# Attention in a transformer layer: the ones and value matmuls of two key tiles issued together, ones first, after one wait

## What is computed

```python
def attn(x):                                  # x is layer-normed
    qkv = x @ Wqkv                            # q: 32 heads x 128, k: 128, v: 128
    scores = einsum('bqhd,bkd->bhqk', q, k) * 128 ** -0.5
    alibi = slopes[h] * (pos_k - pos_q)       # slopes fall from head 0 to head 31
    scores = where(pos_k <= pos_q, scores + alibi, -1e30)
    return einsum('bhqk,bkd->bqhd', softmax(scores), v) @ Wo
x = x + layernorm(attn(layernorm(x)))
# feed-forward: three 4096 x 4096 layers with weights +1 / -1 made of booleans
h = relu(s0 * (layernorm(x) @ pm(k0))) * 2
h = relu(s1 * (ei(h) @ pm(k1))) * 2           # ei: the last 819 features times -4
x = x + layernorm(s2 * (ei(h) @ pm(k2)))
```

## Time and profile before

| | us |
|---|---|
| median of two runs | 7135.25 |
| the two runs | 7068.7 and 7201.79 |
| the profiled execution | 7065.34 |
| its span, from the first to the last instruction on the slowest core (core 1) | 7063.8 |
| spans of the other seven cores | 7047.1 to 7061.9 |
| mean granted TensorE clock, all cores | 0.906 to 0.911 of full speed |

### The profile page before, as it was taken

How to read it: one execution, slowest core, us unless ns; L and a number is a source line. 1 busy time by engine, 2 the same in 40 slices (tenths; PEclk the granted TensorE clock), 3 DMA queues, 4 the chain that set the end, 5 groups by cost and what they waited for, 6 DMA issues and landing times. The chain is left out here.

```text
span 7063.8 us, 68459 instructions; the slowest of 8 cores (7047.1 to 7063.8 us)
## 1 busy us (share of the span) xinstructions
PE 5567.9 (79%) x26898; PEld 2564.7 (36%) x26898; DVE 1513.9 (21%) x1592; ACT 1714.4 (24%) x3454; POOL 416.0 (6%) x492
## 2 busy tenths in 40 slices
PE   1998678981799999990299868888981799999990
PEld 1444333430344444440144423444431344444440
DVE  3001671015110110004300123441015110110004
ACT  3001650005100100003300298881005100100004
POOL 0000000000011110000000000000000011110000
PEclk9999999995899999995599989999995899999995
DMA  2543003442344443324344300004542344443324
GB/s 50 77 72 54 1 1 61 77 72 70 65 78 72 75 78 72 78 66 141 61 72 76 45 1 1 1 1 60 74 75 64 70 75 72 78 75 75 76 68 143
DMA packets 491400, 445.22 MB, mean 63 GB/s; under 512 B 9683, under 2 KB 476628, under 8 KB 480852
## 3 DMA queue, kind: packets, MB, share of 16 engines
q0 software_dynamic: 478848, 373.32, 31.3%
q1 hardware_dynamic: 12244, 67.53, 2.8%
HBM read 461.78 MB, written 50.33 MB: 72 GB/s over the span
## 5 line engine op out<-in xcount | busy, mean ns | idle before, releaser
L397 PE MATMUL pb<-wst,A 128*128 128x512 bf16 (+1 forms) x12800 | 2729.3, 376 | 119.7 <-DMA wst<-wo 29.2
L397 PEld LDWEIGHTS pb<-wst,A 128*128 128x128 bf16 x12800 | 1251.8, 98 | 1596.6 <-issue 159.8
L605 ACT ACTIVATE PTs<-pb,eb_sb 128x64 bf16<-128x64 f32 (+4 forms) x2720 | 941.2, 621 | 251.2 <-PE pb L547 151.6
L807 PE MATMUL pb<-Bt,wst 128*128 128x512 bf16 x4096 | 890.1, 381 | 17.1 <-DVE wst L780 17.1
L807 PE MATMUL pb<-A,wst 128*128 128x512 bf16 x4096 | 889.7, 381 | 13.4 <-DVE wst L780 13.3
L505 PE MATMUL pb<-PTs,on 128*128 128x512 bf16 (+2 forms) x1280 | 466.0, 364 | 167.7 <-ACT PTs L605 163.3
L807 PEld LDWEIGHTS pb<-Bt,wst 128*128 128x128 bf16 x4096 | 402.0, 98 | 505.2 <-issue 25.8
L807 PEld LDWEIGHTS pb<-A,wst 128*128 128x128 bf16 x4096 | 401.7, 98 | 500.9 <-issue 21.3
L547 PE MATMUL pb<-QT,KT 128*128 128x512 bf16 (+2 forms) x1280 | 453.0, 370 | 106.8 <-DVE QT L584 72.8
L572 DVE RECIPROCAL DR<-pb 128x512 f32<-128x512 f32 x128 | 429.1, 3352 | 291.3 <-PE pb L510 291.3
L510 PE MATMUL pb<-PTs,Vb 128*128 128x512 bf16 (+2 forms) x1280 | 466.7, 365 | 0.0
(11 more groups left out here) (66 smaller groups left out, 2127.9 us busy)
## 6 DMA issues: line engine op xcount, KB each, us to landing
wst<-k POOLq DMA_DIRECT2D x256, 512.0 KB, 4.2
wst<-wqkv POOLq DMA_DIRECT2D x64, 1024.0 KB, 8.4
wst<-wo POOLq DMA_DIRECT2D x64, 1024.0 KB, 9.5
wst<-k POOLq DMA_DIRECT2D x64, 1024.0 KB, 5.8
oh<-x POOLq DMA_DIRECT2D x32, 1024.0 KB, 9.4
out<-oh SPq DMA_DIRECT2D x32, 1024.0 KB, 6.1
x1sp<-Bt SPq DMA_DIRECT2D x16, 1024.0 KB, 4.3
ln<-x1sp SPq DMA_DIRECT2D x32, 512.0 KB, 5.6
```

Of the source, the lines that this page charges most:

```text
L397: mi = t.matmul(pb[tl][:, 0:Wd], lhsT_get(i, tl), wst[:, n % 2, ii, 0:Wd], start=(i == 0), stop=(i == 31))
L605: i = s.activation(PTs[:, j % 4, off:off + w], pb[4 + j % 3][:, off:off + w], AF.Exp, bias=eb[:, col:col + 1])
L807: mi = t.matmul(pb[pbase + 2 * oc + sh][:, 0:512], wst[:, n % 2, ii, oc * 128:oc * 128 + 128], arena_chunk(src_arena, i)[:, sh * 512: sh * ...
```

## The change

`emit_dpv` is replaced by `emit_dpv_group`, which takes two trips. It waits once, for the exponentials of the later trip of the two, then issues both ones matmuls, then both value matmuls. Trips are collected in the list `pend`, and a group is issued as soon as four are pending, that is behind every second score matmul. What is left at the end of a head is issued in groups of two. The operands, banks, buffers and the number of matmuls stay what they were, and so does every other engine's program.

```diff
-            def emit_dpv(t, j):
-                ...
-                t.wait_ge(sEXP.sem, bEXP + j + 1)
-                di = t.matmul(pb[2 + n % 2][:, qs:512], on1[:, :],
-                              PTs[:, j % 4, 0:Wd], ...)
-                if j == head_last[h]:
-                    di.then_inc(sQf.sem, 1)
-                mi = t.matmul(pb[n % 2][:, qs:512], Vb[:, kt, :],
-                              PTs[:, j % 4, 0:Wd], ...)
-                mi.then_inc(sPV.sem, 1)
+            def emit_dpv_group(t, js):
+                t.wait_ge(sEXP.sem, bEXP + js[-1] + 1)
+                for j in js:
+                    ...
+                    di = t.matmul(pb[2 + n % 2][:, qs:512], on1[:, :],
+                                  PTs[:, j % 4, 0:Wd], ...)
+                    if j == head_last[h]:
+                        di.then_inc(sQf.sem, 1)
+                for j in js:
+                    ...
+                    mi = t.matmul(pb[n % 2][:, qs:512], Vb[:, kt, :],
+                                  PTs[:, j % 4, 0:Wd], ...)
+                    mi.then_inc(sPV.sem, 1)
...
-                        jh0 = j
+                        pend = []
...
                                 mi.then_inc(sST.sem, 1)
-                                if j > jh0 + 1:
-                                    emit_dpv(t, j - 2)
+                                pend.append(j)
+                                if len(pend) >= 4:
+                                    emit_dpv_group(t, [pend.pop(0),
+                                                       pend.pop(0)])
                                 j += 1
-                        if j > jh0 + 1:
-                            emit_dpv(t, j - 2)
-                        emit_dpv(t, j - 1)
+                        while pend:
+                            emit_dpv_group(t, pend[:2])
+                            pend = pend[2:]
```

More of the change, by code:

```diff
@@ L498, in trip_parts @@
                 return h, qloc, kt, qq, qs, Wd, subs, n
-            def emit_dpv(t, j):
-                h, qloc, kt, qq, qs, Wd, subs, n = trip_parts(j)
-                nkt = 4 * qq + 4
-                km = _ktmin(h, qq)
-                t.wait_ge(sEXP.sem, bEXP + j + 1)
-                di = t.matmul(pb[2 + n % 2][:, qs:512], on1[:, :],
-                              PTs[:, j % 4, 0:Wd],
-                              start=(kt == km), stop=(kt == nkt - 1))
-                if j == head_last[h]:
-                    di.then_inc(sQf.sem, 1)
-                mi = t.matmul(pb[n % 2][:, qs:512], Vb[:, kt, :],
-                              PTs[:, j % 4, 0:Wd],
-                              start=(kt == km), stop=(kt == nkt - 1))
-                mi.then_inc(sPV.sem, 1)
+            def emit_dpv_group(t, js):
+                t.wait_ge(sEXP.sem, bEXP + js[-1] + 1)
+                for j in js:
+                    h, qloc, kt, qq, qs, Wd, subs, n = trip_parts(j)
+                    nkt = 4 * qq + 4
+                    km = _ktmin(h, qq)
+                    di = t.matmul(pb[2 + n % 2][:, qs:512], on1[:, :],
+                                  PTs[:, j % 4, 0:Wd],
+                                  start=(kt == km), stop=(kt == nkt - 1))
+                    if j == head_last[h]:
+                        di.then_inc(sQf.sem, 1)
+                for j in js:
+                    h, qloc, kt, qq, qs, Wd, subs, n = trip_parts(j)
+                    nkt = 4 * qq + 4
+                    km = _ktmin(h, qq)
+                    mi = t.matmul(pb[n % 2][:, qs:512], Vb[:, kt, :],
+                                  PTs[:, j % 4, 0:Wd],
+                                  start=(kt == km), stop=(kt == nkt - 1))
+                    mi.then_inc(sPV.sem, 1)
             with nc.Block() as blk:
```

## The result

The changed kernel is slower: 1.0070 times the kernel before, 95% interval 1.0057 to 1.0084, that is 49 us (40 to 59) on the 7068.7 of the faster run before. This is well under the 2% above which the forecast would have called it slower. The forecast was 70 us, which lies above the interval. The profiled execution took 7122.06 us, 57 over that of before.

A forecast was written before the change was run, and what follows sets the result against it. The prediction took ScalarE to pace attention's first heads and TensorE the last twenty of the second half; 57 us at the same clock plus 13 for the clock gave 7135, or 7139 against the faster run, range 7110 to 7180.

The forecast's parts named there:

- The bound of each stage: Second-half attention: ScalarE paces the first heads, TensorE heads 12 to 31; first-half heads 12 to 31: VectorE's evacuations delay turns.
- Part 1, the shared stationary: Two ones matmuls of a group load the same matrix: taken as 0, bounds 0 and a gain of 64 us.
- Part 2, the second exponential: Second-half heads 12 to 31: waiting for two exponentials makes every second group 0.21 us late; 1.6 a head, 32 us.
- First half, heads 12 to 31: VectorE's evacuation wait absorbs the loss at a head's start; 0.4 us a head remains, 8 us for 20 heads.
- Heads 8 to 11: Loop of 3.09 us for four trips against 2.92; 1.85 us a head in second half, 0.5 in first, 9 us.
- Heads 0 to 7: ScalarE never runs dry in the stream; 0.6 us a head in second half, 0.4 in first, 8 us.
- Part 3, the clock: Heads 12 to 31: added idle time lowers TensorE's granted clock; 13 us taken, bounds 0 and 39 us more.
- The sum: Whole kernel: 57 us at the same clock plus 13 us for the clock, 70 us on 7065.3, giving 7135.
- Hidden: Rival: ScalarE hop 0.2 us shorter in the stream, late groups vanish, some 25 us stay: 7090; chance 0.13.
- Faster by fewer waits: Rival: each TensorE wait before ones matmuls costs a fixed price, half go, 84 us less: 6985; chance 0.04.
- Clock: Rival: added idle drops attention's clock, to 0.91 in second half, 0.76 in first; 119 us in all, 7188; chance 0.21.

The follow-up runs named there:

- e3: Changed kernel with its single wait kept, but ones and value matmuls alternating (D P D P) within the group; 7118.3 us at best, no interval.
- e1: Changed kernel with its order kept, but each ones matmul waits for its own trip's exponentials alone; 7075.1 us in one execution.
- e4: Kernel before with its order kept, but the first ones matmul of each pair waits for the later trip's exponentials; 1.0342 times the kernel before, 7300 us.
- e6: Changed kernel with groups issued at six pending trips instead of four and eight exponential buffers instead of four; 1.0060 times the kernel before.
- e8: Changed kernel with the wait for VectorE's evacuation moved to a query block's first ones matmul, as in e5; 1.0024 times the kernel before.
- e9: Changed kernel's groups in one stream across heads, evacuation wait at the first ones matmul; 0.9897 times the kernel before.
- e5: Kernel before with the wait for VectorE's evacuation moved from a query block's first score matmul to its first ones matmul; 0.9924 times the kernel before.

## Why the prediction was right, point by point

**The bound of each stage** was read rightly. The late heads of the second half carry 37 of the 64 us in the profile, the ones bound by ScalarE (heads 0 to 7 there) 5.

**Part 1, the shared stationary, 0.** Right, and e3 tests it apart from the rest: 21.41 us with D P D P, 21.42 with D D P P.

**Part 2, the second exponential.** Forecast for a second-half head of tier 512: five late groups of 0.21, two starts of 0.36, 0.2 given back, 19.77 to 21.4. Measured 21.42, with each piece at its place in the timeline: 0.36 late at the start and again at the turn, five late groups (0.22 us three times and 0.26 twice, the latter where the tiles are narrow, 1.2 in all), and the 0.22 us wait before the head's last D gone. Taking the wait back removes 1.40 of 1.65 us (e1), putting the wait alone into the old order makes a clean head 26.02 (e4), and giving the loop two more trips makes 20.20 (e6). In total 20 x 1.65 = 33 us, forecast 32.

**First half, heads 12 to 31.** Forecast 0.4 a head, measured 11.52 - 11.13 = 0.39. That VectorE's wait takes in a part of the price is shown by e8, and in the head itself: the wait at the turn, 1.51 us before, is now

```profile
863.89 0.59 PE L552 MATMUL pb<-QT,KT 128*128 128x512 bf16 x2 [1.15 <-DVE A L582]
```

It is shorter by 0.36, what the start loses.

**Heads 8 to 11.** Forecast 7.4 and 2 us, measured 6.5 and 1.0.

**Heads 0 to 7.** Forecast 8 us in all, measured 3.5 + 1.9 in the second half and 2.4 + 6.5 in the first, 14. The second half fits (5 forecast); heads 0 to 3 of the first half lost 6.5 us where 1.6 was put. On this core the time at half clock rose there from 35 to 52 us, and the forecast had looked for the clock only in heads 12 to 31. But the clock is only a part of it: on cores 2, 4 and 6 that time was 45 us before and 41 to 45 after, and the same heads lost 3.2 to 3.6 us all the same. So some 3 us are the clock and some 3 a cost that the forecast put at 1.6; what it consists of is open.

**Part 3, the clock, 13 us.** The direction was right. In heads 12 to 31 of the second half the clock now falls in 9 of 20, nearly every second head, before in 5 (6 to 9 and 1 to 5 over the cores). Two neighbouring heads after, 20 and 22 us of them:

```profile
4571.00:4591.00 20.00, 17.57 (x87) 7.73 (x88) 8.65 (x5) 16.11 (x28) 0.00 (x0) 1.00 0.00 0
4592.00:4614.00 22.00, 19.58 (x92) 8.22 (x89) 8.70 (x5) 16.22 (x28) 0.00 (x0) 0.92 0.00 1
```

The first keeps the full clock (1.00) and lasts 21.42 us, the second (0.92) 4614.48 - 4591.59 = 22.89. But what it costs was mis-sized. Over those 20 heads the time beyond clean heads went from 405.8 - 395.4 = 10.4 to 442.6 - 428.4 = 14.2 us, 4 more, and in the first half from 12.5 to 10.5, 2 less. With some 3 us of heads 0 to 3 it is 5 us where 13 were put. The forecast took each us at half clock as dear as before (11/16 of a us); it became cheaper. The time at half clock in the second half's heads went from 17 to 31 us and in the first half's from 41 to 55, but the time lost only from 10.4 to 14.2 and from 12.5 to 10.5. That TensorE does part of its slower work while it would wait for ScalarE anyway is a likely reason, and not shown.

**The sum.** 57 + 13 were forecast; attention grew by 62 us (mean of eight cores), the profiled execution by 57, and the timed ratio says 40 to 59. Against attention itself the forecast is 8 us too high (6 against the 64 of core 1). On core 1 the clock term was put 8 us too high and heads 8 to 11 2 too high, while heads 0 to 7 were put 3 too low, so two errors cancel in part, which is luck. Another 5 us are the untouched phases, which ran that much shorter in the profile; the forecast had taken it that attention's time shows in full. What stands between 57 and the ratio's 49 was not followed; 57 lies near the upper end of the interval.

**The rivals.** *Hidden* fails: the hop is as long in the stream as at a head's start, and the late groups are there. *Faster by fewer waits* fails: in e4 every second wait is met long before and the kernel is 3.4% slower, and e1, with twice the waits of the changed kernel, is faster than it. *Clock* as a main cause fails: the clock stood at 0.97 in heads 12 to 31 of the second half, and clean heads, without any fall, carry 41 of the 62 us. The rule in the Trainium skill, "TensorE: Matmul & The Clock Gate", section "A second HAM failure mode: psum-queue depth-cycling", on brief pauses between groups at N=512 is not borne out inside the stream: the head above waits at every second group and holds 1.00 throughout, and in e9, with the same groups and no break between heads, the clock never fell in heads 12 to 31 of either half.

## What to carry to other kernels

When two engines hand tiles back and forth, write down the loop: what must pass between issuing a producer and the consumer's wait, hop by hop, against the slots that the engine has of its own in between. Merging two waits moves the wait to the later of the two events, and it is free only if the slack is longer than one more tile of the other engine (0.58 us here, against 0.15 us of slack and one extra slot of 0.22). And a wait should stand at the instruction that needs it: moving one past the score matmuls brought 47 us in the first half, and that together with filling the breaks between heads brought the kernel to 0.9815 of its time.

## What was not expected

The granted clock is a second price of idle time, and of where it lies. In e5 the first half's heads 12 to 31 went from 41 to 7 us at half clock when a 1.5 us wait a head was moved and shrank to 0.53; in e6 a wait of 2.27 us in place of 1.51 took the same heads to a granted clock of 0.75. Neither size was foreseen; for the change itself the clock's part came to less than half of the forecast, some 5 us where 13 were put.
